# Interleaving a tile's columns by four, with reordered transposes and loads, in a fused conditional-linear and mixture kernel

## The reference

```python
x = x + (einsum('bsd,bdh->bsh', x, W[cat_ids]) + b[cat_ids][:, None, :])          # L0
h = gelu(einsum('bnd,hd->bnh', x, fc1_w) + fc1_b)                                 # fc1, 2048 hidden
shared   = einsum('bnh,sh->bns', h, fc2_w) + fc2_b                                # 384 columns
expert_x = einsum('bnh,bph->bnp', h, experts_w[indices]) + experts_b[indices]     # 128 columns
x = x + concatenate([shared, expert_x], axis=-1)                                  # fc2
```

## Time and profile before

| | us |
|---|---|
| median of 3 timed runs (1678.97 to 1681.01) | 1680.95 |
| the profiled execution's own time | 1681.4 |
| its span in the trace | 1679.6 |
| TensorE busy | 1639.4 (98%) |
| VectorE busy | 1176.4 (70%) |
| ScalarE busy | 551.9 (33%) |
| DMA engines' mean busy share, 153.28 to 1581.21 us | 0.70 |

### The profile page before, as it was taken

The page is one execution under the profiler, slowest core; times in us unless marked ns, Lnnn a source line. Parts: engine busy times, 40 slices in busy tenths (PEclk is TensorE's granted clock), DMA queues, the critical chain, the costliest instruction groups (busy, mean ns, idle before and its releaser), DMA issues.

```text
span 1679.6 us, 28015 instructions
## 1 busy us (share of the span) xinstructions
PE 1639.4 (98%) x7065; PEld 1315.8 (78%) x7065; DVE 1176.4 (70%) x2004; ACT 551.9 (33%) x927; POOL 195.1 (12%) x195
## 2 busy tenths in 40 slices
PE   7899999999999999999999999999999999999999
PEld 5778887877878778787877878778787787878887
DVE  5677667776777767776776677767777677767754
ACT  4343333333323333333332333333333333333321
POOL 0200100111020010200102001110200102001110
PEclk9999999999999999999999999999999999999999
DMA  7886776757677575775767767686775757757630
GB/s 207 185 190 150 147 149 147 156 129 162 127 163 151 131 156 118 167 159 133 149 133 160 156 144 157 131 157 135 163 153 131 155 118 164 163 131 151 134 61 26
DMA packets 884826, 243.44 MB, mean 145 GB/s; under 512 B 803688, under 2 KB 818168, under 8 KB 884732
## 3 DMA queue, kind: packets, MB, share of 16 engines
q1 hardware_dynamic: 740732, 203.75, 57.1%
q10 hardware_dynamic: 144000, 38.82, 10.7%
HBM read 209.93 MB, written 32.51 MB: 144 GB/s over the span
## 4 chain that ended last, share of the span: by engine, by line
PE 66%; SPq 20%; issue 8%; DMA 3%; DVE 2%; ACT 1%; DVEq 0%
PE ps_out L814 30%; PE ps_h L799 14%; PE ps_e L799 13%; PE ps_y L786 8%; SPq L386 8%; SPq L341 4%; SPq L320 2%; DMA e_blocks<-in_L_cond_experts_w 2%; SPq L399 2%; SPq L351 1%; SPq L393 1%; PE ps_t L745 1%; DVE e_whole L643 1%; DVE h L599 1%; DVE w2e L599 1%
## 5 line engine op out<-in xcount | busy, mean ns | idle before, releaser
L814 PE MATMUL ps_out<-w2e,h 128*128 128x512 f32 x3072 | 758.0, 396 | 10.0 <-DVE h L599 10.0
L814 PEld LDWEIGHTS ps_out<-w2e,h 128*128 128x128 f32 x3072 | 574.3, 188 | 152.5 <-DVE h L599 15.9
L799 PE MATMUL ps_e<-y_t,w 128*128 128x512 f32 x1536 | 376.8, 395 | 1.4 <-DVE y_t L599 1.4
L799 PE MATMUL ps_h<-y_t,w 128*128 128x512 f32 x1536 | 375.7, 394 | 0.0
L799 PEld LDWEIGHTS ps_e<-y_t,w 128*128 128x128 f32 x1536 | 290.7, 189 | 66.9 <-DVE y_t L599 1.6
L799 PEld LDWEIGHTS ps_h<-y_t,w 128*128 128x128 f32 x1536 | 288.5, 188 | 65.7
L643 DVE STREAM_TRANSPOSE e_whole<-e_blocks 128x512 f32<-128x512 f32 x256 | 182.0, 711 | 109.3 <-DMA e_blocks<-in_L_cond_experts_w 100.9
L530 ACT CAST w2e<-e_whole 128x512 fp32r<-128x512 f32 x256 | 158.6, 620 | 284.4 <-PE ps_out L814 157.4
L463 POOL TENSOR_TENSOR x_raw<-x_raw,b_all 128x512 f32<-128x512 f32 x60 | 85.3, 1422 | 1354.9 <-DMA x_raw<-in_x 1303.2
L499 ACT CAST w_split<-w_raw 128x512 fp32r<-128x512 f32 x244 | 145.7, 619 | 243.7 <-DMA w_raw<-in_L_cond_W 174.4
L599 DVE TENSOR_TENSOR w_split<-w_raw,w_split 128x512 fp32r<-128x512 f32 x244 | 161.1, 688 | 84.6 <-ACT w_split L499 83.7
(11 more groups left out here) (71 smaller groups left out, 431.3 us busy)
## 6 DMA issues: line engine op xcount, KB each, us to landing
e_blocks<-in_L_cond_experts_w SPq DMA_DIRECT2D x1024, 64.0 KB, 2.9
w_raw<-in_L_cond_W SPq DMA_DIRECT2D x248, 256.0 KB, 2.9
out<-resid SPq DMA_DIRECT2D x64, 256.0 KB, 4.7
x_blocks<-in_x SPq DMA_DIRECT2D x240, 64.0 KB, 2.4
b_all<-in_L_cond_b SPq DMA_DIRECT2D x60, 256.0 KB, 4.3
x_raw<-in_x SPq DMA_DIRECT2D x60, 256.0 KB, 4.6
y_rows<-y ACTq DMA_DIRECT2D x60, 256.0 KB, 2.8
x_blocks<-y_rows ACTq DMA_DIRECT2D x240, 64.0 KB, 3.7
```

The source lines that it names most:

```text
L799: last = nc.tensor.matmul(h_bank(c)[:, :], w1[:, w, k, c * P:(c + 1) * P], y_t[:, a, k, :, :].rearrange("p b s -> p (b s)"), start=(k == 0 ...
L814: last = nc.tensor.matmul(ps_out[b][:, :], h[:, c % 2, a, b * S:(b + 1) * S], fc2_columns(c, c % 2, w, b), start=(c == 0 and n == 0), stop ...
```

## The change

**Data layout.** A tile of 128 contraction indices is no longer 128 neighbours but every fourth one of 512: tile k holds the units k, k+4, k+8, and so on. The L0 weights are loaded with the same row order (row 4p+k goes to partition p), fc1's rows likewise, so the sums are over the same products in another order. A row's piece in a block DMA is then 128 neighbours (512 bytes) where it was 32 (128 bytes), and the step of four moves into the transposes, on VectorE (L614, L627, L643) and TensorE (L745): they read every fourth element. The piece count of an expert or x block DMA falls from 512 to 128. fc2's preparation tiles are read in whole 2 KB rows, and the bias `b1` is loaded in place, without transpose.

```diff
+        def every_fourth(whole, k):
+            return whole.rearrange("p (m k) -> p k m", k=KD)[:, k]
...
-                return fc2_w[n * P:(n + 1) * P, :].rearrange("p (k u h) -> u p k h", k=QUAD, h=P)[q]
+                return fc2_w[n * P:(n + 1) * P, q * QUAD * P:(q + 1) * QUAD * P]
...
-                            .rearrange("o (j q) (c u i r) -> u i q c (o j) r", q=Q, c=QUAD, i=P // Q, r=Q)[quad, i]
+                            .rearrange("o (j q) (u i n) -> u i q (o j) n", q=Q, i=P // Q, n=P)[quad, i]
...
-                nc.vector.transpose(x_whole_t[:, :], x_blocks[:, :]).then_inc(x_turned, 1)
+                nc.vector.transpose(split_of(x_whole_t[:, :]), blocks_of(x_blocks[:, :])).then_inc(x_turned, 1)
...
-                off = (c % QUAD) * P
-                nc.vector.transpose(e_whole[:, :], e_blocks[:, (c // QUAD) % 2, :, off:off + P]).then_inc(e_turned, 1)
+                src = e_blocks[:, (c // QUAD) % 2, :, :].rearrange("p b (j r c) -> p c (b j) r", c=QUAD, r=Q)[:, c % QUAD]
+                nc.vector.transpose(e_whole[:, :].rearrange("p (a q) -> p a q", q=Q), src).then_inc(e_turned, 1)
...
-                turn(prep_bank(t), [prep_tile(t)[:, n * P:(n + 1) * P] for n in range(4)]).then_inc(prep_turned, 1)
+                turn(prep_bank(t), [every_fourth(prep_tile(t), k) for k in range(KD)]).then_inc(prep_turned, 1)
```

```diff
-    L0_STEPS = (1, 3, 5, 7, 9, 10, 11, 12)
+    L0_STEPS = (2, 3, 5, 7, 9, 10, 11, 12)
...
-                    if c > 0:
-                        turn_next_e(g, c, more)
                     h_high(g, c)
                     prep_low(prep_in_step(g, c, 0))
                     h_low(g, c)
-                    if c == 0:
-                        turn_next_e(g, c, more)
+                    turn_next_e(g, c, more)
                     prep_low(prep_in_step(g, c, 1))
                     if more:
-                        if c == 0:
+                        if c == L0_STEPS[0] - 1:
                             turn_x(g + 1, 0)
```

More of the change, by code:

```diff
@@ L361, in load_l0_in @@
             def load_l0_in(G, c):
-                for b, step in ((0, 0), (1, 1), (2, L0_STEPS[1] + 3), (3, L0_STEPS[3] + 3)):
-                    if c == step:
-                        load_x_blocks(G, b)
                 for p in range(2 * GB):
@@ L375, in load_l0_in @@
                         load_x(G, b)
+                for b, step in ((0, 0), (1, L0_STEPS[0]), (2, L0_STEPS[1] + 3), (3, L0_STEPS[3] + 3)):
+                    if c == step:
+                        load_x_blocks(G, b)
             def load_experts(g, quad, idx, batches, blocks=range(P // Q)):
@@ L429, in body @@
                         load_l0_in(g + 1, c)
-                    if c == 0 and not first(g):
-                        store(g - 1)
                     b, quad = (c + 1) % GB, (c + 1) // QUAD + 1
@@ L438, in body @@
                         load_experts(g + 1, quad - NC // QUAD, next_idx, [b])
-                    if first(g) and c == 0:
+                    if c == 0 and not first(g):
+                        store(g - 1)
+                    if first(g) and c == 1:
                         sp.dma_start(b2_all[:, :], fc2_b.rearrange("(o n) -> o n", o=1).to_broadcast([P, SHARED]))\
@@ L597, in _, with split_of, blocks_of @@
         def _(dve):
+            def split_of(whole_t):
+                return whole_t.rearrange("p (k j q) -> p k j q", k=KD, q=Q)
+            def blocks_of(blocks):
+                return blocks.rearrange("p (j r k) -> p k j r", k=KD, r=Q)
             def minus(dst, whole, high):
@@ L626, in turn_y @@
                 dst = (y_hold[:, 0, :], y_hold[:, 1, :], x_whole_t[:, :], ps_t[:, :])[b]
-                nc.vector.transpose(dst, x_blocks[:, :]).then_inc(y_turned, 1)
+                nc.vector.transpose(split_of(dst), blocks_of(x_blocks[:, :])).then_inc(y_turned, 1)
             def y_sum(G, b):
```

51 lines of the change are left out of this document (21 added, 30 removed).

## The result

The changed kernel takes 1656.7 us (median of four timed runs, 1651.6 to 1660.2) against 1681.0 for the kernel before: a ratio of 0.985, 95% interval 0.983 to 0.988. The forecast was 1657 in a range of 1649 to 1671. The profiled execution took 1658.0 us, its span is 1656.2.

What follows compares the result with a forecast made beforehand. TensorE, busy 1639.4 of 1679.6 us, was taken as the bound, so only its gaps or added work count. 1681.4 - 20 (middle groups) - 7 (first group) + 3 (TensorE's strided reads) = 1657.4, said as 1657; range 1649 to 1671.

Steps and rivals of the forecast that it cites:

- TensorE's stalls, put at 21.1 us: 14 middle groups: 1427.93 us against 1406.9 if all matched the first; nearly all waits on h and x_t; -20 taken.
- Wait A goes: First L0 pair's wait on x_t, 9.6 us in 12 waits, vanishes with the pair one step later; slack over 4 us.
- Wait B goes in either case: Step 4's fc2 wait on h's low half, 10.0 us in 13 waits, vanishes with or without cheaper DMA issues.
- My 0.25 us a DMA: SyncE's x-block and expert DMAs: saving per issue with fewer pieces, some 5 us over 20, nothing if pieces don't set the price.
- rival 3: Waits move to steps 2 and 3, or step 4 waits again; half of the 20 us stays: 1667 us, chance 0.10.
- the estimate of 1120 from the pace of casts: VectorE's strided transpose: 1120 ns if slowed by the 1.6 between cast and transpose; rounded up to 1420 as upper bound.
- two of the prediction's own signs of being wrong: Profile after: expert transposes of 1 us or more; preparation transposes over 0.09 us apart, lengthening 36 to 153 us.
- The wait on y_t that was to follow the first: TensorE waiting at a group's first fc1 on y_t, expected if expert transposes took 1 us or more.
- My bound for a stall: Group's end on VectorE: transposes about 1.25 us start to start push y past fc1, up to 0.4 us a group.
- -7 forecast: First group: -6 for the 3.40 us wait and its low clock, -1 for a preparation DMA wait; 0.3 us from b1.
- +3 forecast: TensorE's strided transposes in preparation, x and y tiles: a quarter more taken; the 23 step tiles 0 to 8.3 us.
- the 2.6 us that the clock was to give: First group, 69 to 76 us: loss from the 0.63 granted clock behind the 3.40 us gap, expected to go.

Runs made afterwards that it cites:

- 3: Kernel before with only the expert's transpose moved behind h's low half in every step; ratio 1.029 to the kernel before.
- 7: Changed kernel with the expert's transpose put back ahead of h in steps 1 to 15; ratio 0.985 to the kernel before.
- 1: Kernel before with all order edits but the old layout, 128-byte pieces and contiguous transposes; ratio 0.999 to the kernel before.
- 2: Changed kernel with all order edits taken back, so the new layout alone; ratio 0.994 to the kernel before.
- 12: Changed kernel with SyncE's old order (x blocks ahead of slices, store ahead of experts, first biases in step 0); 1674 us, ratio 0.995 to the kernel before.
- 11: Changed kernel with the first L0 pair, its x transpose and second x blocks moved back to their earlier steps; ratio 1.042 to the kernel before.
- experiment 5: Changed kernel with VectorE's transposes reading neighbouring elements, so its output differs; 1651.6 us, ratio 0.982 to the kernel before.
- 8: Changed kernel with the b1 load moved behind the last L0 weight slice of the first group; 1657.7 us, ratio 0.985 to the kernel before.
- 10: Changed kernel with both L0 weight slices of a pair in one DMA from the second group on; 1658.8 us, ratio 0.986 to the kernel before.
- experiment 9: Kernel before with all order edits and strided VectorE transposes, old 128-byte pieces, output not the reference's; ratio 1.026 to the kernel before.
- experiment 6: Changed kernel with each of SyncE's expert and x block DMAs issued as two of half the size; ratio 1.099 to the kernel before.

## Why the prediction was right, and which of its steps were not

**The bound was read rightly.** All that the middle groups could give was TensorE's stalls, put at 21.1 us. They gave 24.6: the idle time of 19.8 us (1427.93 less 1408.18) fell to 0.5, and the busy time for the same matmuls fell by 5.3 us (1402.85 against 1408.18). The restarts behind the stalls are in these 5.3 us. The forecast had 1.5 us for them, and what the rest is was not looked into.

**"Wait A goes", by a slack of over 4 us: right in the outcome, wrong in the working.** The pair was due 14 us after fc1, as forecast. But the slices did not go out 3 us earlier: they left 3.5 us after fc1, and in the kernel before it was 3.6 us after it. I moved them to the head of SyncE's list and kept the head where it was. The turn behind h moved the head itself. The transpose that frees the quad slot starts 9.2 us ahead of the next fc1 (452.02), where before it started 12.4 us ahead of the 361.93 of the earlier trace rows:

```profile
349.55 0.71 DVE L643 STREAM_TRANSPOSE e_whole<-e_blocks 128x512 f32<-128x512 f32 x1
```

The experts' DMAs and the biases follow it, and from the last bias to the next head SyncE takes 7.5 us here (457.19 to 464.66) and 6.1 to 7.0 in the kernel before, in 3 and in 7. Experiments 3 and 7 show that price with nothing else changed: the head goes from 0.3 us before fc1 to 3.0 behind it, and back to 0.2 before. I had followed the move through VectorE's list, and not to who waits for the moved transpose. The x blocks take what is left: 5.5 us from issue to transpose where I took 3. Slack 0.2.

**"Wait B goes in either case", even without cheaper issues: right for the wait, wrong for the time.** On the old pieces (1) the wait on h goes, and the middle groups take as long as before, with waits on w_split and x_t. The layout alone removes it (2). What I had missed is SyncE's issue rate: 0.77 us a block DMA from start to start before, 0.50 after. My 0.25 us a DMA was the right size, but I had given it no part in the sum. Without it the result is rival 3 ("the waits move"), at the full 20 us rather than half. The layout keeps it out, and not by itself: with the layout, the old order of SyncE's list costs 20.4 us (12), the old step of the pair 97.8 (11), and the turn ahead of h nothing (7).

**The transposes: 711 ns forecast, 1090 measured.** It lies between the bounds and next to the estimate of 1120 from the pace of casts, which I had worked out and not taken. The Trainium skill's rule ("SBUF — State Buffer", Specifications (TRN2): lines of 16 bytes, two hits in each for full bandwidth) has the right sign here, and experiment 5 against the changed kernel gives the size, 703 against 1090 ns; that the lines are the reason was not tested. With it two of the prediction's own signs of being wrong appeared, a transpose above 1 us and preparation transposes more than 0.09 us apart. The wait on y_t that was to follow the first did not come. The end of the group took it, just: y's last half ends 0.13 us ahead of fc1, where 1.1 us were free before. My bound for a stall was 1.25 us start to start; the strided one takes 1.02 (457.59 to 458.61).

**The first group: -7 forecast, -4.4 measured**, and the transposes on TensorE, +3 forecast. The 3.40 us stall of the earlier trace rows and the low clock of 69 to 76 us are gone: the tile that waited there runs without a gap, and the clock over 66 to 80 us is at its full level. The 1.42 us wait for a preparation DMA is gone too.

```profile
66.00:80.00 14.00, 14.00 (x71) 11.74 (x69) 10.89 (x17) 4.58 (x8) 0.96 (x1) 1.00 0.85 217
```

Two stalls ahead of a preparation tile that the kernel before had as well (1.59 us at 42.67, 1.12 at 86.77) are now 2.0 us at 48.83 and 1.4 at 87.63. And the low clock came elsewhere: 0.56 over 41.63 to 47.00 and 0.66 over 49 to 54 us. So the idle time fell nearly as forecast, by 4.1 us (7.5 to 3.5), and the 2.6 us that the clock was to give were not seen. In 5, 8 and 10, with the clock at 0.98 to 1.00 in this stretch, it takes 108.8 to 110.6 us. A preparation tile takes 0.39 us in place of 0.36, so 23 of them are 0.7 us, at the low end of what I gave:

```profile
82.82 0.63 PE L745 MATMUL ps_t<-ident,prep_raw 128*128 128x128 f32 x4
83.21 3.04 PE L812 MATMUL ps_out<-w2e,h 128*128 128x512 f32 x12
```

**The start was taken as unchanged, but for a part of the +3, and lost 5.6 us.** Every kernel on the new layout has its first fc1 at 38.6 to 41.6 us, every one on the old weights' order at 36.0 to 37.8, experiment 9 with strided VectorE transposes among them (37.8) and experiment 5 without them on the other side (40.0). So it isn't VectorE's stride. What the layout adds there is weight slices whose rows lie 8 KB apart, TensorE's strided loads, and `b1` in small pieces. Over the whole kernel the slices land later in the changed one. Before and then after (KB each, median us from issue to landing):

```profile
w_raw<-in_L_cond_W SPq DMA_DIRECT2D x248, 256.0 KB, 2.9
w_raw<-in_L_cond_W SPq DMA_DIRECT2D x248, 256.0 KB, 4.0
```

Some 3 us are the layout's. The rest goes with the clock of this profile: over the start it was granted at 0.89 on average where the kernel before had 1.00, most of it in one stretch, in which TensorE did 21 matmuls where the kernel before did 38 in the same 7 us:

```profile
19.00:26.00 7.00, 6.25 (x21) 4.67 (x20) 5.45 (x9) 3.86 (x7) 0.00 (x0) 0.51 0.99 343
```

That is close to the lower level of 1.2 GHz, and TensorE had been busy for 9.5 of the 19 us ahead of it, against 11.7 in the kernel before. The other profiles on the layout have 0.96 to 1.00 over the start, and 38.6 to 40.4 us. Which of the three, landing, loads or `b1`, costs the 3 us was not tried apart, but for the inconclusive 8.

So the total came right by some luck, from terms that were off in opposite directions: the middle 4.6 us better, the start, first group and TensorE's loads together 5.2 us worse than forecast (+1.2 measured, -4 forecast).

## What to carry to other kernels

An in-order issuing queue is an engine with a busy time of its own. Count its issues by their distance from start to start, and ask of each place whether it waits for others or others for it; a queue that hardly ever waits for a free slot may be the bound even where its name stands in no row of TensorE's waits, and here the chain of work named it, with 20% of the span. When an instruction is moved behind another, follow the buffer that it frees to who refills it, and on to that queue's next group. The same edit can cost 50 us in one setting and nothing in another: here the turn behind h (3 against 7) and the stride (9 against 5).

## What the hardware showed that I had not expected

- The price of a DMA issue on SyncE's queue fell from 512 to 128 pieces and not from 128 to 64: from start to start 0.77 us with 512 pieces (kernel before), 0.50 with 128 (changed kernel), 0.50 with 64 (experiment 6), by the medians of the traces.
- A transpose on VectorE that reads every fourth 4-byte element takes 1090 ns, 1.53 to 1.55 times the 711 or 703 of one that reads neighbours; a 128 by 128 weight load on TensorE 206 ns against 143, 1.44 times, of which 0.03 us a tile of four comes to light.
- 256 KB slices of 128 pieces of 2 KB land in 4.0 us where the rows lie 8 KB apart in HBM, against 2.9 us in one run of addresses, by the medians of both kernels; on the old weights' order the three order experiments have 2.8 to 2.9, and on the new one layout alone has 3.9.
- Waits of 3.9 or 4.9 us a group are paid for again: in experiment 3 the same matmuls take 18 us longer, in 11 they take 29 us longer, at a granted clock of 0.98 in both.
